# The state's fading on TensorE, its copy on ScalarE, and the gate's logits split in two

## What is computed

```python
# attention, by chunks of C tokens, W is the state of one head
inter = einsum('bij,bcj->bci', W, rk_c) * g_p
S     = einsum('bcd,bkd->bck', rk_c, wk_c)
intra = einsum('bck,bkd->bcd', S * M, v_c)
W_new = g_C * W + einsum('bci,bcj->bij', v_c * g_w, wk_c)
reads = alpha * (inter + intra)
x     = x + n(x) + reads @ W_read.T            # n is the layer norm
# experts
z      = n(x)
logits = z @ gate_w.T
probs  = softmax(logits); top 2 of 8
out    = x + sum over the two of prob * (gelu(z @ w1 + b1) @ w2 + b2)
```

## Time and profile before

| | us |
|---|---|
| median of 3 runs | 559.88 |
| lowest, highest | 559.78, 563.1 |
| profiled execution | 562.67 |
| its span, first to last instruction | 560.9 |
| TensorE busy | 530.1 (95%) |
| VectorE busy | 448.4 (80%) |
| ScalarE busy | 338.3 (60%) |
| GpSimd busy | 246.9 (44%) |
| mean granted TensorE clock | 0.99 |

### The profile page before, as it was taken

One profiled execution on the slowest core, in us unless ns is written; L12 is line 12 of the kernel. 1 busy time (PEld: TensorE's weight loads), 2 busy tenths in 40 slices (PEclk: granted clock), 3 DMA queues, 4 the chain that ended last, 5 costly groups with the idle time before them and its releaser, 6 DMA issues.

```text
span 560.9 us, 17645 instructions
## 1 busy us (share of the span) xinstructions
PE 530.1 (95%) x5234; PEld 415.3 (74%) x5234; DVE 448.4 (80%) x1375; ACT 338.3 (60%) x856; POOL 246.9 (44%) x291
## 2 busy tenths in 40 slices
PE   7799899999999999999999999999999999999991
PEld 7677778778786777777777777777777777777770
DVE  4889999999987689868768787688777777778861
ACT  6899989898745876445545554455544544545540
POOL 5625778888746084523223233223322333322433
PEclk9999999999998999999999999999999999999997
DMA  5576867777345396433263364343344454344323
GB/s 161 201 229 225 258 185 234 210 222 231 126 105 129 87 216 101 71 60 62 51 103 56 53 105 77 63 68 61 61 63 79 78 78 75 68 64 67 63 37 36
DMA packets 85096, 63.33 MB, mean 113 GB/s; under 512 B 54224, under 2 KB 77392, under 8 KB 85008
## 3 DMA queue, kind: packets, MB, share of 16 engines
q1 hardware_dynamic: 71328, 43.94, 32.3%
q0 software_dynamic: 13392, 18.27, 17.3%
q10 hardware_dynamic: 288, 0.00, 0.0%
HBM read 37.56 MB, written 24.62 MB: 111 GB/s over the span
## 4 chain that ended last, share of the span: by engine, by line
PE 77%; DVE 10%; issue 4%; DMA 3%; ACT 2%; POOL 1%; SPq 1%; POOLq 0%; DVEq 0%; ACTq 0%
PE psum L1697 32%; PE psum L1712 21%; PE psum L1714 10%; PE psum L1509 3%; DVE weights L874 2%; PE psum L1592 2%; PE psum L1573 2%; PE psum L1599 2%; PE psum L1520 2%; DVE arena L1052 1%; PE psum L1559 1%; DMA arena<-sent_rows 1%; PE psum L1612 1%; PE psum L1496 1%; DVE arena L1063 1%
## 5 line engine op out<-in xcount | busy, mean ns | idle before, releaser
L1697 PE MATMUL psum<-arena,weights 128*128 128x256 f16 (+1 forms) x2208 | 279.7, 249 | 1.1 <-DVE arena L1316 1.0
L1697 PEld LDWEIGHTS psum<-arena,weights 128*128 x2208 | 187.4, 98 | 79.3 <-issue 4.1
L589 POOL DMA_INDIRECT out<-arena,tile_in x71 | 115.0, 1619 | 233.4 <-DVE arena L1343 126.9
L1712 PE MATMUL psum<-weights,arena 128*128 x556 | 211.7, 381 | 0.0
L826 ACT ACTIVATE arena<-psum,b_cur 128x256 f32<-128x256 f32 (+1 forms) x368 | 131.4, 423 | 129.9 <-PE psum L1697 115.6
L1714 PE MATMUL psum<-weights,arena 128*128 x556 | 152.0, 273 | 0.0
L1327 DVE TENSOR_TENSOR arena<-arena 128x512 f16<-128x512 f32 x142 | 98.5, 694 | 10.8 <-ACT arena L843 6.3
L559 POOL DMA_INDIRECT sent_rows<-arena,tiny x64 | 65.4, 1022 | 35.5 <-issue 17.8
L1323 DVE CAST arena<-arena 128x512 f16<-128x512 f32 x126 | 53.5, 424 | 8.8 <-ACT arena L826 8.5
L1712 PEld LDWEIGHTS psum<-weights,arena 128*128 128x128 f16 x556 | 54.4, 98 | 5.0
L1714 PEld LDWEIGHTS psum<-weights,arena 128*128 128x128 f16 x556 | 54.5, 98 | 4.6
(11 more groups left out here) (199 smaller groups left out, 642.9 us busy)
## 6 DMA issues: line engine op xcount, KB each, us to landing
weights<-in_experts SPq DMA_DIRECT2D x32, 512.0 KB, 4.8
arena<-sent_rows SPq DMA_DIRECT2D x100, 64.0 KB
arena<-in_b SPq DMA_DIRECT2D x46, 128.0 KB, 3.2
arena<-in_x SPq DMA_DIRECT2D x16, 256.0 KB, 3.4
out<-arena SPq DMA_DIRECT2D x16, 256.0 KB, 4.1
arena<-sent_rows SPq DMA_DIRECT2D x84, 32.0 KB
sent_rows<-pad SPq DMA_DIRECT2D x7, 265.0 KB, 4.6
tile_in<-sent_rows SPq DMA_DIRECT2D x71, 4.5 KB, 2.6
```

Of the source, the lines that this page charges most:

```text
L589: pool.indirect_dma_start(out=out, out_offset=bass.IndirectOffsetOnAxis(ap=at_u, axis=0), in_=yout[:, u % 4], in_offset=None, compute_op=A ...
L1697: last = pe.matmul(ps_h[:, f % 2, mm * n:(mm + 1) * n], w1_of(e_of[i], k, lo, per * (f - GROUP[i]) + mm), turned[:, i % 2, part, k, 0:n], ...
L1712: pe.matmul(to, h_hi[:, z % 4, at], w2_of(e_of[t], m), start=(m == 0), stop=(m == MF - 1), skip_group_check=True)
```

## The change

The names are those of the diff.

- **The gate's logits are made without the normed rows.** The gate's weights are centred once (`mean_gate`, `centre_gate`) so that the mean of a row drops out, and 1/deviation is applied later, as the scale of the exponential. Since x1 is the first residual plus `reads @ W_read.T`, the logits are a sum of two parts: `gate_x` (TensorE, from the transposed f16 halves of the chunk, scaled by `scale_gate` on ScalarE) and eight more columns of `project`, whose weights hold `W_read` times the gate (`gate_through_reads`, `read_gate`, once at the start, with one more DMA of 256 KB). `logits` on VectorE adds the two. `turn_normed`, `score_experts` and ScalarE's `normed_transposed` are gone.
- **The logits come one step earlier**, for chunk n-3, so the choice and the sending are for chunk n-4 (`LAG` = 4).
- **The state's fading is on TensorE.** Behind the products of `states`, two f32 products of a diagonal matrix (`fade`, made once by `fade_tables`) with the old state add onto the same PSUM. `carry` is now one copy of 128 x 256 from PSUM, on ScalarE.
- **GpSimd** makes the factor that `scale_gate` uses, by two tiny operations (`roots`, `sides`) after its two chains.
- In the order of the steps, `gate_x(n-3)` is first on TensorE, ahead of `turn_chunk`; `carry(n-3)` and `scale_gate(n-3)` stand on ScalarE between `chunk_residual` and `exponential`; `logits(n-3)` stands on VectorE between `residual` and the first `split_low`.
- PSUM banks are given out anew, and the small parts of the last chunks are moved accordingly: no transposes and no gate products stand between the expert pairs any more.

The diff, cut to its core:

```diff
-LAG = 5
+LAG = 4
...
+                if active(n, 0):
+                    reached(pool, "gate_x_done", n - 4)
+                    pool.tensor_tensor(roots[:], ve1, rs1[par], ALU.mult).then_inc(S["root_done"], 1)
+                    reached(pool, "root_done", n)
+                    pool.tensor_scalar(sides[:, n % 4], roots[:], 1.0 / WSCALE, 1.0 / WSCALE, ALU.mult,
+                                       ALU.add).then_inc(S["side_done"], 1)
...
-            def normed_transposed(m):
-
-                reached(a, "mT_ps", m)
-                reached(a, "logit_ps", m - 1)
-                a.activation(xmT.rearrange("p b k t -> p (b k t)"), ps_mT.rearrange("p b k t -> p (b k t)"),
-                             ACT.Copy).then_inc(S["mT_done"], 1)
+            def carry(m):
+
+                reached(a, "state_ps", m)
+                reached(a, "read_ps", m)
+                reached(a, "gate_x_ps", m)
+                a.activation(state.rearrange("p b k i -> p (b k i)"), ps_state.rearrange("p b k i -> p (b k i)"),
+                             ACT.Copy).then_inc(S["state_done"], 1)
+
+            def scale_gate(m):
+
+                reached(a, "gate_x_ps", m)
+                reached(a, "side_done", m)
+                reached(a, "logit_done", m - 1)
+                for b in range(B):
+                    last = a.activation(gate_x_part[:, b], ps_gate_x[:, b], ACT.Copy, scale=sides[:, m % 4, b:b + 1])
+                last.then_inc(S["gate_x_done"], 1)
...
-                a.activation(shifted, shifted, ACT.Exp).then_inc(S["exp_done"], 1)
+                reached(a, "rs2_done", m)
+                for b in range(B):
+                    last = a.activation(shifted[:, b], shifted[:, b], ACT.Exp, scale=rs2_of(m)[:, b:b + 1])
+                last.then_inc(S["exp_done"], 1)
...
-                if active(n, 5):
-                    exponential(n - 5)
+                if active(n, 3):
+                    carry(n - 3)
+                    scale_gate(n - 3)
+                if active(n, 4):
+                    exponential(n - 4)
                 if 1 <= n < NCH:
                     chunk_keys(n - 1)
                 for j in splits(n)[1:2] if len(splits(n)) > 2 else ():
                     split_high(j)
...
-                if active(n, 4):
-                    normed_transposed(n - 4)
...
-                reached(v, "logit_ps", m)
+                reached(v, "proj_ps", m)
+                reached(v, "gate_x_done", m)
                 reached(v, "top_at_done", m - 1)
-                v.tensor_copy(logit, ps_logit).then_inc(S["logit_done"], 1)
+                v.tensor_tensor(logit, ps_gate_read, gate_x_part[:], ALU.add).then_inc(S["logit_done"], 1)
...
-            def carry(m):
-
-                reached(v, "state_ps", m)
-                reached(v, "read_ps", m)
-                reached(v, "state_done", m - 1)
-                for k in range(KD):
-                    last = v.scalar_tensor_tensor(out=state[:, :, k], in0=state[:, :, k], scalar=decayC[:, k:k + 1],
-                                                  in1=ps_state[:, :, k], op0=ALU.mult, op1=ALU.add)
-                last.then_inc(S["state_done"], 1)
...
-                if active(n, 5):
-                    largest(n - 5)
-                if active(n, 3):
-                    carry(n - 3)
+                if active(n, 4):
+                    largest(n - 4)
                 if active(n, 0):
                     moments(n)
-                if active(n, 5):
-                    choose(n - 5)
+                if active(n, 4):
+                    choose(n - 4)
                 if active(n, 1):
                     chunk_low(n - 1)
                 if active(n, 1):
                     chunk_queries(n - 1)
                 if active(n, 3):
                     residual(n - 3)
+                    logits(n - 3)
                 for j in splits(n)[0:1]:
                     split_low(j)
                 if active(n, 3):
                     residual_stats(n - 3)
-                if active(n, 5):
-                    weigh_gates(n - 5)
+                if active(n, 4):
+                    weigh_gates(n - 4)
                 if active(n, 3):
                     residual_moments(n - 3)
                 if active(n, 2):
                     weigh_scores(n - 2)
-                if active(n, 5):
-                    place(n - 5)
                 if active(n, 4):
-                    logits(n - 4)
+                    place(n - 4)
...
+            def centre_gate():
+
+                v.wait_ge(gate_mean_ps, 1)
+                v.tensor_tensor(gateT[:], gateT[:], ps_gate_mean.unsqueeze(1).to_broadcast([P, KD, E]),
+                                ALU.add).then_inc(gate_centred, 1)
+
+            def gate_in_halves():
+
+                v.wait_ge(gate_centred, 1)
+                v.tensor_scalar(gate16[:, 0], gateT[:], WSCALE, None, ALU.mult).then_inc(gate_halves, 1)
+                v.wait_ge(gate_halves, 1)
+                v.scalar_tensor_tensor(out=gate16[:, 1], in0=gateT[:], scalar=WSCALE, in1=gate16[:, 0], op0=ALU.mult,
+                                       op1=ALU.subtract).then_inc(gate_halves, 1)
+
+            def fade_tables():
+
+                v.wait_ge(setup_act, 7)
+                for k in range(KD):
+                    v.tensor_scalar(fade[:, k], ident, decayC[:, k:k + 1], None, ALU.mult).then_inc(fade_done, 1)
+
+            def read_gate():
+
+                v.wait_ge(wr_gate_ps, 1)
+                v.tensor_copy(wrT[:, :, D:D + E], ps_wr_gate).then_inc(wr_gate_done, 1)
...
+            def gate_through_reads():
+
+                pe.wait_ge(gate_centred, 1)
+                pe.wait_ge(rows_in, 16)
+                for k in range(KD):
+                    for j in range(KD):
+                        last = pe.matmul(ps_wr_gate[:, k], wr_rows[:, j, k * P:(k + 1) * P], gateT[:, j],
+                                         start=(j == 0), stop=(j == KD - 1))
+                last.then_inc(wr_gate_ps, 1)
+
+            def gate_x(m):
+
+                s = m % 2
+                reached(pe, "gate_x_done", m - 1)
+                reached(pe, "state_done", m - 1)
+                reached(pe, "xlo_done", m)
+                if m == 0:
+                    pe.wait_ge(gate_halves, 2)
+                for b in range(B):
+                    for at, (k, x, w) in enumerate(three):
+                        last = pe.matmul(ps_gate_x[:, b], xnT[:, x, s, b, k, 0:P], gate16[:, w, k],
+                                         start=(at == 0), stop=(at == len(three) - 1))
+                last.then_inc(S["gate_x_ps"], 1)
...
-                        last = pe.matmul(ps_proj[:, b], readsT[:, s, b, k, 0:P], wrT[:, k], start=(k == 0),
+                        last = pe.matmul(ps_both[:, b], readsT[:, s, b, k, 0:P], wrT[:, k], start=(k == 0),
...
+                if m == 0:
+                    pe.wait_ge(setup_pool, 2)
+                    pe.wait_ge(fade_done, KD)
                 for b in range(B):
                     for h in range(H):
                         d, cols = slice(h % 2 * HD, (h % 2 + 1) * HD), slice(h * HD, (h + 1) * HD)
-                        last = pe.matmul(ps_state[d, b, h // 2], keys[:, s, b, cols], vals[:, b, cols],
-                                         start=True, stop=True)
+                        pe.matmul(ps_state[d, b, h // 2], keys[:, s, b, cols], vals[:, b, cols],
+                                  start=(b == 0 and h < 2), stop=True, skip_group_check=True)
+                for k in range(KD):
+                    last = pe.matmul(ps_state[:, :, k], fade[:, k], state[:, :, k], start=False, stop=True,
+                                     skip_group_check=True)
                 last.then_inc(S["state_ps"], 1)
...
+                if active(n, 3):
+                    gate_x(n - 3)
                 if active(n, 1):
                     turn_chunk(n - 1)
                 if active(n, 3):
                     project(n - 3)
-                if active(n, 4):
-                    turn_normed(n - 4)
                 if active(n, 2):
                     values(n - 2)
                 if active(n, 2):
                     weigh(n - 2)
-                if active(n, 5):
-                    rank(n - 5)
+                if active(n, 4):
+                    rank(n - 4)
                 if 2 <= n <= NCH:
                     states(n - 2)
-                if active(n, 4):
-                    score_experts(n - 4)
                 if active(n, 2):
                     reads(n - 2)
...
             pair(0, None)
             pair(1, None)
             project(NCH - 1)
-            turn_normed(NCH - 2)
             pair(2, None)
-            rank(NCH - 3)
-            score_experts(NCH - 2)
+            rank(NCH - 2)
             pair(3, 0)
-            rank(NCH - 2)
+            rank(NCH - 1)
             pair(4, 1)
-            turn_normed(NCH - 1)
             pair(5, 2)
-            score_experts(NCH - 1)
             pair(6, 3)
```

(1 more changed line is left out.)

## The result

The changed kernel takes 577.43 us (median of 4 runs, 574.23 to 580.89) against 561.49 (4 runs, 559.78 to 564.59) for the kernel before, run beside it: ratio 1.0279, 95% interval 1.0199 to 1.0359. It is slower, as forecast, but by 15.9 us and not by 10.7, and so lies just above the range (577.0). Medians here are of fast executions: one of e4's four (583.19 us) was slow and is left out of its median.

What follows compares the result with a forecast made beforehand. A ring of hand-overs between TensorE, ScalarE and VectorE was taken to bound each chunk step. Start and steps 12.6 us later, less 1.9 in the drain, gave 10.7 on 559.88: forecast 570.5 us, range 563 to 577.

Steps and rivals of the forecast that it cites:

- the new wait: On VectorE, `logits(n-3)` waits for ScalarE's scaled `gate_x`, ahead of the first `split_low`; idle about 0.6 us a step.
- the two rings: Chunk loop: Ring A at 10.72 us and Ring B at 11.02 us, taken as the length of a step.
- the drain: After the chunk loop: one transpose group (0.44), one `score_experts` (0.99) and half of another (0.5) go; 1.9 us back.
- the start: Up to `reads(1)`: diagonals, `gate_through_reads` and `gate_x` come ahead of the transposes; `reads(1)` at 31.06, not 28.28.
- the last step: Last step of the chunk loop, without a weight piece: 8.64 us, ending at 169.54 against 156.94.
- rival 3: GpSimd's loop, held by VectorE's weight pieces, becomes the bound: 11.4 us in all eight two-piece steps, 576 us; chance 0.12.
- rival 4: TensorE's clock falls; in every step it would double 3.5 us of Ring A: over 600 us; chance 0.03.
- Ring A: Chunk step from `reads` through `gate_x`, ScalarE's scalings, VectorE's logits and weight piece to the next `reads`: 10.72 us.
- rival 2: Same wait but short, with `gate_x` at 0.46 and the copy at 0.21: Ring A 10.34, 565.0 us; chance 0.15.
- Ring B: Three-piece steps, from `reads` through ScalarE's copy, keys and values to `states` and the diagonals: 11.02 us.
- The steps: Chunk loop: four steps at 11.02 bring `reads` to 75.14, eight at 10.72 to 160.90, against 147.20.
- One hold alone, 10.2: Within rival 3: GpSimd's loop with only one operation held by a VectorE piece takes 10.2 us, below Ring A.

Runs made afterwards that it cites:

- e4: Changed kernel with GpSimd's two added operations done once, using the first chunk's factor for all, instead of in each step; 575.44 us, ratio 1.0242.
- e15: Changed kernel with TensorE's wait ahead of `states` filled with idle products and GpSimd's two operations done once, scaling left late; 571.34 us, ratio 1.0177.
- e2: Changed kernel with TensorE's wait ahead of `states` filled with products that nobody reads; 575.54 us, ratio 1.0253.
- The square: Changed kernel with TensorE filled, scaling late or early, GpSimd's operations every step or once: e2 575.54, e15 571.34, e16 576.83, e11 567.9 us.
- e11: Changed kernel with TensorE filled, ScalarE's copy and scaling early, and GpSimd's two operations done once; 567.9 us, ratio 1.0112.
- e13: Changed kernel with early copy and scaling, root and side on VectorE, TensorE filled and the end order of e5; 568.99 us, ratio 1.0128.
- e14: e13 with the state part undone, so `carry` is on VectorE again without products with diagonals; 566.17 us, ratio 1.0079.
- e16: Changed kernel with TensorE filled and ScalarE's copy and scaling early, GpSimd's two operations kept in every step; 576.83 us, ratio 1.0288.
- e1: Changed kernel with `carry(n-3)` and `scale_gate(n-3)` on ScalarE moved ahead of the first `split_high` and `chunk_residual`; 581.49 us, ratio 1.0327.
- e3: Changed kernel with the state part undone: fading and sum on VectorE again, gate part kept; 572.81 us, ratio 1.0179.
- e5: Changed kernel with another end order: `residual(15)` and `logits(15)` ahead of `split(1)` and `low_tile(1)`, `scale_gate(15)` ahead of `gelu(0)`; 577.34 us, ratio 1.026.
- e9: Changed kernel with VectorE's weight piece made from one SBUF input, the subtraction left out; 574.34 us, ratio 1.0242.
- e7: Kernel before with the state part alone: `carry` a copy on ScalarE, fading by TensorE products with the diagonals; 566.6 us, ratio 1.0109.

## Why the prediction came out as it did

The direction, the new wait and its place were right; the size was 5.2 us short. The step that failed is the one that takes the length of a step from the two rings alone ("Four at 11.02 bring `reads` to 75.14, eight at 10.72 to 160.90"). GpSimd's held loop and the falls of TensorE's clock stand at nothing in that sum, each put off as a rival, and they came to 6.3 us. Second to it, the drain gave back 0.9 us of 1.9.

By the spans of the profiled executions the change is 14.6 us against 10.7 forecast, 3.9 more: 0.3 in the start, 2.3 in the three-piece steps, 0.5 in the last step and 1.0 in the drain, less 0.2 in the two-piece steps. The other 1.3 of the 5.2 comes of comparing medians with single executions: the profiled one of the kernel before lies 1.2 above its median, that of the changed kernel does not.

Of the recorded signs, VectorE's idle time before the logits came (0.55). The distance of 10.6 to 11.1 came in the three-piece steps only (10.78) and not in the two-piece ones (10.31 to 10.39). The signs of rival 3, ScalarE waiting over 1 us for `shift2` and GpSimd without a wait, and of rival 4, a clock under 1 before 160 us, came as well. The steps of the forecast, one by one:

**Ring A: right, one term too large.** In the undisturbed step from 111.38 to 121.69 the logits start 6.60 behind `reads` (forecast 7.02) and `reads` 3.71 behind them (forecast 3.70). The 0.42 is one term: `gate_x`, taken at 0.75 between 0.46 and 1.49. It takes the lower end, 0.46, until its result is there, and only 0.32 stand ahead of the transposes, which start before it has ended. The lower end had been read from a row with 128 columns and was the one to believe. Ring A is 10.31, not 10.72, and e15 shows it alone. That is the ring of rival 2 (10.34): on this term the rival was right, and its time (565.0) was wrong all the same. The copy (0.27 for 0.30) and the scalings (0.46 for 0.42) were right.

**Ring B: right.** 10.78 against 11.02, with `gate_x` 0.43 shorter and the diagonals longer, 0.64 for 0.55. It holds in the undisturbed three-piece steps of every kernel that has both parts, whether the scaling is early or late.

**The start: right in the sum.** `reads(1)` comes at 31.35 (forecast 31.06), but in other parts. The interval is 12.36, not 13.17, and `reads(0)` is 1.10 late, because the clock granted from 12 to 20 us was 0.64 and made `weigh` and `values` last 1.66 and 2.30 where they take 0.98 and 1.49 in the kernel before. In e15 that stretch was at full clock, and `reads(0)` came at 18.29, 0.40 late. TensorE at the start (line 1632 `weigh`, 1646 `values`), with `reads(0)` and `reads(1)`:

```profile
14.41 1.66 PE L1632 MATMUL psum<-arena 64*128 64x128 f16 x24 [0.48 <-DVE arena L1081]
16.01 2.30 PE L1646 MATMUL psum<-ww,arena 128*128 128x256 f16 x12
18.99 1.09 PE L1665 MATMUL psum<-arena 128*64 128x128 f32 x16 [0.69 <-ACT arena L740]
...
31.35 0.91 PE L1665 MATMUL psum<-arena 128*64 128x128 f32 x6
```

**The steps: the size failed.** Against the forecast the four three-piece steps are 2.25 longer and the eight two-piece steps 0.21 shorter. Four steps of ring B are 43.12; a clock fall adds 1.60 (12.38 for 10.78, gone in e2) and GpSimd's held step 1.61. Eight of ring A are 82.48; a held step adds 1.17, a clock fall 1.54 (11.92 for 10.38, gone in e2), and the excess of GpSimd's loop over the ring the remaining 0.36. So 4.2 us of ring that I had too much were more than covered by 6.3 us that I had not at all (1.60, 1.61, 1.17, 1.54 and 0.36). That the total came as near as it did is the luck of two errors of opposite sign.

**Rival 3 was a part, not a rival.** "One hold alone, 10.2, leaves it below the ring" is the sentence that failed: the loop was 10.39 and the ring 10.31. GpSimd in the two-piece step, against the earlier trace rows: chain, `roots` (578), `sides` (580), first send:

```profile
122.19 1.06 POOL L575 TENSOR_TENSOR tiny<-tiny,rs_slots 128x2 f32<-128x2 f32 x1
123.21 0.19 POOL L578 TENSOR_TENSOR roots<-tiny 128x2 f32<-128x2 f32 x1
123.49 0.19 POOL L580 TENSOR_SCALAR sides<-roots 128x2 f32<-128x2 f32 x1
124.29 1.08 POOL L589 DMA_INDIRECT sent_rows<-arena,tiny  x1 [0.61 <-issue]
...
129.24 0.52 POOL L570 TENSOR_SCALAR tiny<-tiny 128x2 f32<-128x2 f32 x1
```

The two operations last 0.19 each, less than taken, but the first send now starts 1.08 behind the start of `roots` where it had followed the chain by 0.17: 0.9 us, not 0.6. About half of that is the gap ahead of the send. It is 0.17 to 0.28 behind a held operation and 0.61 behind one that is not held, in the kernel before too (its next first send starts at 109.77, 0.61 behind a chain that ended free), and now the two operations stand where the hold ended. The holds are 0.86 and 0.30, together 1.16 where they were 1.40. 9.74 + 0.91 - 0.24 = 10.41, measured 10.39. With ring A lower than forecast, that is enough to set the step, by 0.08; and where the pieces come to lie otherwise, in the step from 65.29 and the one from 87.98, by 1.2 to 1.6. The square puts a number on it: 4.2 us of the changed kernel's loss go with these two operations (of the 4.0 at `reads(14)`, 0.8 is the start, where e15's clock happened to be full, and 3.2 the steps). I had the mechanism, priced it as all or nothing, and gave it 0.12.

**Rival 4 also was a part.** I had it as every step or none. It came in the start and in three steps, one of them hidden behind GpSimd, and e2 takes back 3.1 us at `reads(14)` of the profiled execution, 1.9 of the median (the latter not clear of the noise). For the filling as the cure speaks more than e2: all six filled kernels (e2, e11, e13, e14, e15, e16) were granted 1.00 from 31 to 172 us, and all six others with the gate part (the changed kernel, e1, e3, e4, e5, e9) had falls there, one profiled execution each. What the filling doesn't reach is the start: e13 and e14 had `reads(0)` at the fallen clock.

**The last step**: 9.14, not 8.64. Without pieces the ring no longer ends it; TensorE's own work does, with 0.28 us idle before `project` and 0.14 before `reads`. I took the pieces off the ring without asking what is next.

**The drain: failed.** The 1.9 was to come back, 0.9 did (first pair 15.54 later, span 14.6). TensorE, ScalarE and VectorE at the end (before, TensorE waited 1.20 at that place):

```profile
183.16 2.79 PE L1777 MATMUL psum<-arena,weights 128*128 128x256 f16 x24 [0.91 <-DVE arena L1351]
...
191.69 0.17 PE L1606 MATMUL psum<-late_mask,before 128*128 128x16 bf16 x1 [2.65 <-DVE tiny L1057]
```

```profile
187.80 0.41 ACT L678 ACTIVATE gate_x_part<-psum,sides 128x8 f32<-128x8 f32 x2
```

```profile
190.07 0.68 DVE L1351 TENSOR_TENSOR arena<-tileT,arena 128x512 f16<-128x512 f32 x1
...
191.28 0.16 DVE L1057 TENSOR_TENSOR tiny<-psum,gate_x_part 128x16 f32<-128x16 f32 x1
```

The work that I counted as gone is gone, but `rank(14)` waits 2.65 for the logits of chunk 15 (`rank` and `project` write the same PSUM bank), and these stand behind `low_tile(1)` (line 1351) on VectorE. Their scaling, behind `gelu(0)` and `normalise` on ScalarE, had ended at 188.21 and was not what held them. I took two groups of TensorE's work off the sum without following the wait behind them. e5 shows that the order alone doesn't cure it: the next `rank` waits as long.

**The parts of the change.** Alone the state part costs 4.8 us (e7); taken out of the changed kernel it gives 4.6 (e3), and out of e13 2.8 (not clear of the noise). It is dear where ScalarE's values end TensorE's wait, in the start and the three-piece steps. The rest, some 11 us, is by subtraction the gate part: the late scaling, GpSimd's operations, the longer start, and the falls of the clock. What is still open: e14 keeps 5.3 us of it without the late scaling and without GpSimd's operations. By the table it is 5.6 late at `reads(14)`: 0.6 at `reads(0)`, 2.9 in the first interval, 1.4 in the three-piece and 1.1 in the two-piece steps, less 0.4 in the last. No run took these apart (a fall of the clock is in the first interval: e14's `reads(0)` lasts 1.97).

## To carry to other kernels

When the bounds of a step lie close together (here 9.74, 9.84, 10.31 and 10.39), give none of them away as a rival: the step is the longest of them, and each is worth only what it stands above the next. They also move: releasing the ring brought VectorE's pieces onto other operations of GpSimd and lifted its loop from 10.39 to 10.84. So an edit that releases one (e1) can show nothing or a loss until the other is gone as well (e11), and two edits have to be tried as a square. When work is taken off TensorE at the end of a stage, follow the wait that was behind it before you count the gain.

## What the runs showed of the hardware

- Twelve f16 products with 128x128 weights and 8 columns take 0.46 us until done and 0.32 until the next group starts, 0.027 each. The two f32 products with the diagonals (four rows of 128 columns) take 0.71, and 0.64 to the next group (0.55 in e7).
- A weight piece on VectorE holds not only GpSimd's small operations but also its indirect DMAs: a send of 0.96 lasts 1.66 to 1.72 when the piece falls on it. The Trainium skill ("SBUF — State Buffer", section "SBUF: two separate sides") says that GpSimd can't write DMA descriptors while VectorE runs a copy in a mode that takes the shared port pair. The piece here is no such copy but an instruction with two inputs, for which the same page of the Trainium skill (section "Who interferes with whom") infers that it leaves the writing of descriptors free. The measurement decides: the send was held. No run shows which part of it was.
- The one-input piece in e9, 0.68 us long, holds GpSimd too (1.15 for 0.72).
- TensorE waits 1.88 to 2.07 us ahead of `states` in each of the changed kernel's first five steps behind `reads(0)`. Behind two of these waits (30.10 and 64.03) the granted clock fell to 0.57, behind the others it stayed at 1.00. A third fall (0.66 from 98 to 103 us) came behind a shorter wait, 0.92 at 97.74, with one of 1.38 at 92.36 before it. The kernel before, whose longest wait from 20 to 110 us is 1.29, had 1.00 throughout there; it had 1.00 from 12 to 20 us too, with a wait of 2.05 ahead of 14.80. So no length of a single wait in these traces tells a fall from none. With the waits filled (e2) there was no fall. It differs from execution to execution: from 12 to 20 us e15 had 1.00 where e2 had 0.79, with the same instructions up to there on TensorE.
